# Attention with the probabilities turned by DMA transposes of two fp16 halves instead of by TensorE

## The reference, cut to what matters

```python
q = (x @ Wq).reshape(b, lq, H, DK).transpose(0, 2, 1, 3)
kv = (y @ Wkv).reshape(b, lkv, 2, H, DK).transpose(2, 0, 3, 1, 4)
k, v = (kv[0], kv[1])
atten = jax.nn.softmax(jnp.einsum('bhid,bhjd->bhij', q, k) * SCALE, axis=-1)
res = jnp.einsum('bhij,bhjd->bhid', atten, v)
res = res.transpose(0, 2, 1, 3).reshape(b, lq, H * DK)
out = res @ Wproj + bproj
```

## Time and profile before

| | |
|---|---|
| median of 3 runs | 3374.56 us (3371.89 to 3380.78) |
| profiled execution, its own time | 3373.66 us |
| its span | 3371.6 us |
| granted TensorE clock, mean | 0.972 |
| busy share PE / PEld / DVE / ACT / POOL | 91% / 61% / 63% / 53% / 28% |
| first and last addition to X (line 693) | 239.8 us and 2550.6 us |

### The profile page before, as it was taken

One profiled execution on the slowest core, in us unless ns is written; L12 is line 12 of the kernel. 1 busy time (PEld: TensorE's weight loads), 2 busy tenths in 40 slices (PEclk: granted clock), 3 DMA queues, 4 the chain that ended last, 5 costly groups with the idle time before them and its releaser, 6 DMA issues. The chain is left out here.

```text
span 3371.6 us, 72486 instructions
## 1 busy us (share of the span) xinstructions
PE 3077.0 (91%) x27524; PEld 2053.9 (61%) x27524; DVE 2115.1 (63%) x4407; ACT 1776.3 (53%) x3522; POOL 941.7 (28%) x1018
## 2 busy tenths in 40 slices
PE   4999999999999999999999999999996557768998
PEld 3666667666766666676667667666764221145665
DVE  4666566656666665656565665656564659945665
ACT  2545454545455454545454454545453658815665
POOL 2141222222221322222222313222200238825553
PEclk8999999999999999999999999999998779988999
DMA  4111111111111211111111102111002000002111
GB/s 149 35 60 34 47 35 35 35 36 35 35 37 35 60 35 46 35 35 35 36 35 35 44 27 68 33 40 35 16 1 71 0 10 1 1 22 65 55 57 46
DMA packets 70375, 131.29 MB, mean 39 GB/s; under 512 B 6800, under 2 KB 52496, under 8 KB 69744
## 3 DMA queue, kind: packets, MB, share of 16 engines
q1 hardware_dynamic: 70000, 126.23, 12.9%
HBM read 122.02 MB, written 4.19 MB: 37 GB/s over the span
## 5 line engine op out<-in xcount | busy, mean ns | idle before, releaser
L428 PE MATMUL psum<-yT,Q 128*128 128x512 f16 (+1 forms) x5120 | 982.5, 333 | 14.5 <-issue 13.0
L452 PE MATMUL psum<-yN,pT 128*128 128x384 f16 (+1 forms) x3328 | 836.5, 326 | 0.0
L454 PE MATMUL psum<-yN,pT 128*128 128x192 f16 (+1 forms) x3328 | 815.1, 246 | 0.0
L645 DVE TENSOR_TENSOR pT<-psum,pT 128x512 f16<-128x512 f32 (+1 forms) x1024 | 578.6, 587 | 262.8 <-ACT pT L555 248.4
L555 ACT ACTIVATE pT<-psum 128x512 f16<-128x512 f32 (+1 forms) x1024 | 498.7, 514 | 433.0 <-PE psum L440 431.1
L428 PEld LDWEIGHTS psum<-yT,Q 128*128 128x128 f16 x5120 | 448.1, 98 | 384.7 <-issue 18.5
L338 POOL CAST yT<-stage 128x1601 f16<-128x1601 f32 x32 | 48.7, 1522 | 1825.7 <-DVE On L670 1785.5
L633 DVE TENSOR_REDUCE mx<-psum 128x1 f32<-128x1024 f32 (+1 forms) x512 | 481.9, 978 | 50.9 <-PE psum L428 32.2
L440 PE MATMUL psum<-ident,prob 128*128 128x128 f32 (+1 forms) x3328 | 502.2, 277 | 10.9 <-ACT prob L547 10.5
L547 ACT ACTIVATE prob<-psum,nb 128x1601 f32<-128x1601 f32 x256 | 408.6, 1596 | 194.7 <-DVE nb L637 194.7
L440 PEld LDWEIGHTS psum<-ident,prob 128*128 128x128 f32 (+1 forms) x3328 | 362.8, 140 | 150.3 <-DVE pT L645 93.4
(11 more groups left out here) (162 smaller groups left out, 3785.3 us busy)
## 6 DMA issues: line engine op xcount, KB each, us to landing
stage<-in_ctxT SPq DMA_DIRECT2D x32, 800.5 KB, 4.3
stage<-in_ctxT SPq DMA_DIRECT2D x64, 400.2 KB
stage<-in_ctxN SPq DMA_DIRECT2D x32, 672.0 KB, 3.9
wnat<-in_WF SPq DMA_DIRECT2D x32, 512.0 KB, 4.2
stage<-in_ctxN SPq DMA_DIRECT2D x32, 480.0 KB
X<-in_x SPq DMA_DIRECT2D x1, 2048.0 KB, 8.2
Wk<-in_WkS SPq DMA_DIRECT2D x1, 2048.0 KB, 16.4
x_rows<-X SPq DMA_DIRECT2D x1, 2048.0 KB, 8.2
```

What stands on the lines that cost most here:

```text
L428: ins = pe.matmul(psS[:, lo:hi], Q[u][:, q, b, tt * P:(tt + 1) * P], yT[b][:, y, lo:hi], start=(n == 0), stop=(n == 4))
L452: pe.matmul(psO[:, 0:2 * CTX], pT[0][0:k, n, :], yN[b][0:k, n, :], start=(n == 0), stop=False)
L454: ins = pe.matmul(psO[:, 0:CTX], pT[1][0:k, n, :], yN[b][0:k, n, 0:CTX], start=False, stop=(n == JN - 1))
L645: dve.tensor_tensor(pT[1][0:w, lo:hi, :], psT[g % 2][0:w, 0:(hi - lo) * P].rearrange("p (n h) -> p n h", h=P), pT[0][0:w, lo:hi, :], ALU.s ...
```

## The change

The 13 turns on TensorE go. Both halves are made before the turning, side by side with the queries on partitions, and SyncE turns each with one DMA transpose from SBUF to SBUF.

- VectorE copies prob to the fp16 tile ph (`high`, new line 585, between the maxima of one tile and of the next); the 63 columns behind 1601 hold zeros.
- GpSimd subtracts ph from prob and writes the fp16 tile pl (line 392). Before, it only cut the context.
- SyncE turns ph to hT and pl to lT (lines 352 and 354), 128 x 1664 fp16 each. ph and pl are single, hT and lT double.
- `gather` runs two tiles behind the scores (BEHIND = 2) instead of one. `turn_o` comes three tiles behind, before it.
- The context is cut in 8 pieces per batch element instead of 4, one piece per tile, through three staging buffers of 801 columns. On SyncE one piece's load follows each tile's two transposes.
- The turned O has a bank of its own (psT), and so has the projection (psP), which goes by one eighth in each of the last 4 and the first 4 tiles of a pair. psM serves the queries alone.
- The loops are gone: all 256 tiles are written out.
- ScalarE's `high` and VectorE's `low` go.

```diff
-        stage = [sb(f"stage{i}", [P, J]) for i in range(2)]
+        JH = 801
+        PIECES, RING = 8, 3
+        stage = [sb(f"stage{i}", [P, JH]) for i in range(RING)]
         prob = sb("prob", [P, J])
-        pT = [sb(f"pT{i}", [P, JN, P], F16) for i in range(2)]
+        ph = sb("ph", [P, JN * P], F16)
+        pl = sb("pl", [P, JN * P], F16)
+        hT = [sb(f"hT{i}", [P, JN, P], F16) for i in range(2)]
+        lT = [sb(f"lT{i}", [P, JN, P], F16) for i in range(2)]
...
+            for G in range(NT):
+                if G >= 2:
+                    sp.wait_ge(summed, G - 1)
+                sp.wait_ge(hi_kept, G + 1)
+                sp.dma_start_transpose(hT[G % 2][:, :, :], ph[:, :]).then_inc(hi_turned, 16)
+                sp.wait_ge(lo_kept, G + 1)
+                sp.dma_start_transpose(lT[G % 2][:, :, :], pl[:, :]).then_inc(lo_turned, 16)
+                if G + PIECES + 2 < B * PIECES:
+                    load(G + PIECES + 2)
...
+            for G in range(NT):
+                pool.wait_ge(hi_kept, G + 1)
+                if G:
+                    pool.wait_ge(lo_turned, 16 * G)
+                pool.tensor_tensor(pl[:, 0:J], prob[:, :], ph[:, 0:J], ALU.subtract).then_inc(lo_kept, 1)
+                if G + PIECES + 1 < B * PIECES:
+                    cut(G + PIECES + 1)
...
+            def gather(G):
+                b = G // HP % 2
+                if G:
+                    pe.wait_ge(normed, G)
+                pe.wait_ge(hi_turned, 16 * (G + 1))
+                pe.wait_ge(lo_turned, 16 * (G + 1))
...
+            for G in range(NT + BEHIND + 2):
+                p, t = divmod(G, 16)
+                if G < NT:
+                    score(G)
+                if BEHIND + 1 <= G < NT + BEHIND + 1:
+                    turn_o(G - BEHIND - 1)
+                if BEHIND <= G < NT + BEHIND:
+                    gather(G - BEHIND)
+                if t >= 12 and G < NT:
+                    project(p, t - 12)
+                if t < 4 and p:
+                    project(p - 1, t + 4)
...
+            def exponentials(G):
+                act.wait_ge(biased, G + 1)
+                if G:
+                    act.wait_ge(lo_kept, G)
...
+            def high(G):
+                dve.wait_ge(expd, G + 1)
+                if G:
+                    dve.wait_ge(hi_turned, 16 * G)
+                dve.tensor_copy(ph[:, 0:J], prob[:, :]).then_inc(hi_kept, 1)
```

More of the change, by code:

```diff
@@ L273, in attention @@
         recip = sem("recip")
-        turned = sem("turned")
         hi_kept = sem("hi_kept")
         lo_kept = sem("lo_kept")
+        hi_turned = sem("hi_turned")
+        lo_turned = sem("lo_turned")
         summed = sem("summed")
@@ L290, in attention, with place, transfers, loaded_by @@
         x_added = sem("x_added")
-        AHEAD, LO_AHEAD, CTX_AHEAD = 16, 4, 2
-        GROUPS = [(0, 4), (4, 8), (8, 12), (12, 13)]
+        NT = 16 * NPAIR
+        BEHIND = 2
+        def place(G):
+            p, t = divmod(G, 16)
+            b, tt = divmod(t, HP)
+            return p, t, b, tt
+        def transfers(part):
+            return 2 if part in (2, 3) else 1
+        def loaded_by(K):
+            return 16 * sum(transfers(k % PIECES) for k in range(K % RING, K + 1, RING))
+        def half_cols(part):
+            return slice(0, JH) if part % 2 == 0 else slice(JH, J)
@@ L294, in attention @@
         block = ctx.enter_context(nc.Block())
-        def per_pair(i, u, n, k):
-            return i * (2 * n) + (u * n + k)
         @block.sync
         def _(sp):
[L302 to L322, removed]
@@ new lines, in _ @@
+            for K in range(PIECES + 2):
+                load(K)
+            sp.wait_ge(pad_set, 2)
+            for G in range(NT):
[7 more added lines that the diff above has]
+                    load(G + PIECES + 2)
@@ L324, in _ @@
         @block.gpsimd
         def _(pool):
[L326 to L368, removed]
@@ L371, in _, with q_half @@
+            for K in range(PIECES + 1):
+                cut(K)
+            for G in range(NT):
[5 more added lines that the diff above has]
+                    cut(G + PIECES + 1)
         @block.tensor
         def _(pe):
-            def q_half(pair, half, misc_free):
-                misc_free()
+            def q_half(pair, half):
@@ new lines, in turn_o, with project @@
+            def turn_o(G):
+                pe.wait_ge(normed, G + 1)
+                if G:
+                    pe.wait_ge(o_kept, G)
+                for k in range(2):
+                    ins = pe.transpose(psT[:, k * P:(k + 1) * P], On[:, k * P:(k + 1) * P], ident[:, :])
+                ins.then_inc(o_turned, 1)
+            def project(p, tt):
+                pe.wait_ge(o_kept, 16 * p + HP + tt + 1)
+                if tt == 0 and p:
+                    pe.wait_ge(x_added, p)
+                for n, k in enumerate((2 * tt, 2 * tt + 1, H + tt)):
+                    for m, (o, w) in enumerate([(0, 0), (0, 1), (1, 0)]):
+                        ins = pe.matmul(psP, OT[:, o, k, :], Wvp[:, w, k, :], start=(tt == 0 and n == m == 0),
+                                        stop=(tt == HP - 1 and n == m == 2))
+                ins.then_inc(projected, 1)
@@ new lines, in _ @@
+            q_copy(0)
+            q_copy(1)
+            for g in range(HP):
+                qk_high(g)
+            for G in range(NT + BEHIND + 1):
+                p, t = divmod(G, 16)
+                if G < NT:
+                    exponentials(G)
+                if BEHIND + 1 <= G:
+                    o_copy(G - BEHIND - 1)
+                if BEHIND <= G < NT + BEHIND:
+                    sum_low(G - BEHIND)
+                if t < 10 and p + 1 < NPAIR:
+                    if t < 2:
+                        q_copy(2 * p + 2 + t)
+                    else:
+                        qk_high(HP * (p + 1) + t - 2)
```

421 lines of the change are left out of this document (174 added, 247 removed).

## The result

| | before | changed |
|---|---|---|
| median | 3375.95 us (4 runs) | 2925.87 us (4 runs, 2923.38 to 2926.04) |
| ratio, 95% interval | | 0.8665 [0.865, 0.868] |
| profiled execution, span | 3371.6 us | 2924.2 us |
| interval of two additions to X | 154.05 us (mean of 15) | 126.15 us (middle of the run) |

Of all executions reported here one stands apart: 5327.62 us at a mean granted clock of 0.56, one of four of experiment 1; its cause is not known, the median there still holds it and the ratio does not.

The account below looks back on a forecast made before the run. The prediction took TensorE's own work to bound the attention. From the profiled 3373.7 us it took 16 x 22.7 us for the turns and added 8 us at the end: 3018 us, forecast's own range 2960 to 3100, stated range up to 3750.

Parts of the forecast that it names:

- The likeliest case: Whole kernel: TensorE sets the attention's pace and loses the turns' time; 3018 us, range 2960 to 3100, chance 0.47.
- The turns: Turning prob on TensorE: 1.42 us a tile, 22.7 us a pair, all saved on the bounding engine.
- I keep it: TensorE's idle 2.5 us a pair in the attention: kept in the forecast, its removal used as the lower end.
- Matmuls run above most of that, as the 2.5 us idle show: TensorE's weight loads waiting for VectorE's evictions, 80.2 us in 206 waits: mostly covered by matmuls.
- Drain, 8 us: End of the attention: one more iteration of sums, turn of O and projection without scores beside them, about 8 us more.
- The copies and the subtraction: Per tile: high copy on VectorE 1.05 us, low subtraction on GpSimd 3.22 us; their loop of 6.2 us stays below 8.
- Latency: A transpose's time to landing: 3.7 us taken; up to 4.8 us nothing shows, so the term is 0.
- Occupancy: Queue time per transpose: between 1.47 and 10.3 us; up to 3.5 us nothing shows, so the term is 0.
- B: SyncE's queue becomes the bound from 4.2 us of occupancy a transpose; at 4.9 us 3735 us; chance 0.24.
- C: Transposes go block by block at small-packet cost, 10.3 us each, 21.8 us a tile, about 6500 us; chance 0.12.
- A: GpSimd's low subtraction and its transpose alternate and set the pace at 4.8 to 6.3 us landing; about 3200 us; chance 0.13.
- Two tiles behind: Sums run two tiles behind the scores: covers the transposes' remaining latency, costs about 8 us at the end.

Follow-up runs that it names:

- experiment 1: The kernel before with the attention's loops written out, nothing else: 3345.14 us, ratio 0.991.
- experiment 5: The changed kernel with 13 fp32 turns of the identity put back on TensorE in one block before each tile's scores: 3289.76 us.
- experiment 7: The kernel of experiment 1 with only the first block of each group of turned blocks copied and subtracted (short evictions): 3320.70 us.
- experiment 3: The kernel before with loops written out and without turning the probabilities, sums reading constant tiles: 2955.61 us, ratio 0.8759.
- experiment 11: The changed kernel with four extra 7-block DMA transposes a tile, each waiting for the one before: 4454.26 us, ratio 1.3201.
- experiment 12: The changed kernel with the low half's transpose done twice, the second after the first landed, everyone waiting for the second: 3545.02 us.
- experiment 10: The changed kernel with two extra 7-block DMA transposes a tile, one behind each real one: 3019.10 us, ratio 0.8954.
- experiment 8: The changed kernel with the sums one tile behind the scores instead of two: 3387.63 us, ratio 1.0036.

## Why the prediction was right and wrong

**The likeliest case came true in kind, and its gain was put too small.** TensorE alone sets the pace, and the turns' price was right. What failed are the two steps that left the rest of TensorE's time as it was: the idle time that was kept, and the waits for evictions that were put at nothing. With the drain and some small terms they are the 92 us.

- *The turns* (22.7 us a pair) were priced rightly: 22.9 in the ledger, 364 us when put back (experiment 5).
- *"I keep it"*, of the idle 2.5 us a pair: this is the first step that failed. The loops' share of it (2.0 us a pair, 30 us in experiment 1) goes with the loops, as I had half expected and put in the lower end; the wait at a pair's first tile (0.95 in the ledger) goes too, by my reading because the sums of two tiles back cover it, which no run tests. The second was not thought of.
- *"Matmuls run above most of that, as the 2.5 us idle show"*: the second step. Of 5.9 us a pair 1.65 did hold TensorE up (24 us in experiment 7). The profile's busy time could not show it, since ends of matmuls are modelled: busy time counted gaps of 0.1 us as work. The starts of the weight loads, two rows apart in the earlier trace rows, had it: 1.24 us for five loads ahead of the waiting turns, 0.98 for the next five.
- *Drain, 8 us*: none shows. The first addition to X comes 9.7 us later than before, but the last two intervals are 5.6 and 34.9 us shorter than those in the middle, since the last tiles run without scores beside them; 16 pairs at 27.9 us are 446 us, and the span is 447 us shorter.

From 3018: 16 x 2.5 for the idle time, 8 for the drain, 16 x 1.65 for the evictions, 16 x 0.9 for the rest of the ledger, 89 us; measured 92. The last term is 0.2 in the projection, 0.3 in the sums, which go with the turns (experiment 3), and 0.4 between idle time as the page counts it and as the ledger does; the first and third have no experiment that shows them as time.

**The range failed at its narrow end.** I spent it on the side of unknown transposes, up to 3750, and gave the known side 58 us, built from costs that I had measured in the wrong view.

**The copies and the subtraction** were right: 1.04 us for 1.05, 3.23 for 3.22.

**The transposes.** Latency 3.4 us for 3.7 taken. Occupancy: the queue's share times 16 engines is 0.515 x 16 x 2924.2 = 24,095 us, less 6,959 for the loads as before, 17,136 us over 512 transposes and 16 engines, 2.1 us each, at most (see experiment 11 on this share). My bounds were 1.47 and 10.3. The packets are indeed small: 882,688 more of them, 1,724 a transpose, and the trace has 1,664 of 256 bytes for each. But one costs 17,136 / 882,688 = 19 ns, not the 99 ns of the mean packet of 1.8 KB. That is what kept B and C from coming true: the time of a packet was nearer to its bytes than to its number. The Trainium skill's 261 GB/s for a transpose with a non-contiguous middle dimension ("DMA: Bandwidth & Descriptors", "Latency and other measured facts") would be 1.6 us, as an estimate; the trace has 426 KB in 2.1 us, 203 GB/s. Its 1309 ns for one 128x128 block ("VectorE: DVE Perf Modes", "The three transpose paths") doesn't add up block by block: 13 blocks land in 3.4 us.

**Rivals.** A is real, but starts above: at a latency of 6.9 us it costs 619 us (experiment 12). At 3.4 us there is 7.88 - 3.23 - 0.15 - 3.4 = 1.1 us of slack, which the late issue and the longer landing of experiment 10 used up. B as written, occupancy of the queue, was never reached; its neighbours, one queue in which issuing fills SyncE (experiment 10) and one whose waits come in a row (experiment 11), cost 93 and 1,528 us. "Two tiles behind" I had booked only as a drain. The change pays only with it: with one, 3388 us.

## What to carry to other kernels

When an engine is busy 98% and work is taken off it, price the rest by the starts of its instructions, not by its busy share: waits under modelled ends, loop heads and first-tile gaps came to nearly a fifth of the gain here. A change takes some of these waits with it, so give the range room on that side too. A DMA transpose of 128 x 1664 fp16 is worth its place when its result is wanted two tiles later, its source buffer is free again in time (subtraction 3.2 us + landing 3.4 us against the tile's 7.9), and nothing else waits in its queue. A run with the consumer one step nearer tells how much of the gain rests on that distance; here it was all of it.

## What was unexpected of the hardware

- A 256-byte packet of a transpose is given 19 ns; with one and a half times as many moved 23 ns (0.780 x 16 x 3016.4 = 37,645 us, less 6,959, over 1,357,824 packets). The median of the 256-byte packets stays at 18 ns, so that the growth is in some long ones. The high half's landing goes from 3.4 to 5.0 us, and in experiment 12, with three transposes a tile and the DMA queue at 58.9%, it is 5.0 us as well.
- A wait of 2.5 us on TensorE cost as much as 4.1 us in the tile shown: 1.2 us after work began again, the clock fell to half for 3.4 us. In the 207 tiles counted it fell beside 55 of the 78 long waits (experiment 8).
- A fp32 turn of 128x128 between fp16 matmuls costs 0.109 us whether 13 stand together or in pieces of 8, 4 and 1.
- SyncE takes 1.44 us to issue a transpose of 13 blocks in the changed kernel; one of 7 blocks takes 1.2 to 1.6 us in experiment 11's rows, and over 2 us at times in experiments 10 and 11. A plain load takes 0.6.
